# Codes read as they are loaded: the 4-bit levels of one core's second layer without a narrow copy

## What is computed

```python
x = x + _L0_ffn_ref(_L0_cond_ref(x, itok, L0_cond_weights), L0_ffn_w, L0_ffn_b)
x = x + _L1_ffn_ref(_L1_cond_ref(x, L1_cond_weights, itok), q_weight, q_scale, bias, lora_A, lora_B)
# in _L1_ffn_ref
w = NF4_LEVELS[q_weight].reshape(-1, GROUP_SIZE) * q_scale[:, None]
base = jnp.einsum('bsi,oi->bso', x, w) + bias
lora = jnp.einsum('bsr,or->bso', jnp.einsum('bsi,ri->bsr', x, lora_A), lora_B)
return base + SCALING * lora
```

## Time and profile before

| what | us |
|---|---|
| median of three executions | 372.79 |
| the three | 370.15, 373.74, 372.79 |
| the profiled execution, its own time | 371.03 |
| its span in the trace | 369.2 |
| busy in the span: PE, DVE, ACT, POOL | 354.6, 243.3, 169.6, 228.3 |

### The profile page before, as it was taken

One profiled execution on the slowest core, in us unless ns is written; L12 is line 12 of the kernel. 1 busy time (PEld: TensorE's weight loads), 2 busy tenths in 40 slices (PEclk: granted clock), 3 DMA queues, 4 the chain that ended last, 5 costly groups with the idle time before them and its releaser, 6 DMA issues.

```text
span 369.2 us, 5527 instructions
## 1 busy us (share of the span) xinstructions
PE 354.6 (96%) x1832; PEld 299.9 (81%) x1832; DVE 243.3 (66%) x361; ACT 169.6 (46%) x302; POOL 228.3 (62%) x147
## 2 busy tenths in 40 slices
PE   7999987999999999998989999999999999999996
PEld 6788875878888888887868888888888888888885
DVE  4996457587997887974699999846155362544522
ACT  4775647678888778882021323504013040231300
POOL 0769999956886878667443302386468464685642
PEclk9999999899999999999999999999999999999999
DMA  7994400554246146333331133021405014150202
GB/s 212 309 306 142 148 22 29 193 211 146 96 167 199 45 156 216 117 114 114 127 119 57 61 120 114 18 101 62 174 36 180 22 70 166 57 175 4 114 30 85
DMA packets 27838, 44.63 MB, mean 121 GB/s; under 512 B 8834, under 2 KB 17026, under 8 KB 27810
## 3 DMA queue, kind: packets, MB, share of 16 engines
q1 hardware_dynamic: 26466, 43.95, 34.9%
q10 hardware_dynamic: 1344, 0.33, 0.4%
HBM read 27.49 MB, written 16.78 MB: 120 GB/s over the span
## 4 chain that ended last, share of the span: by engine, by line
PE 73%; DVE 10%; ACT 6%; issue 4%; POOL 4%; DMA 1%; SPq 1%; DVEq 0%; POOLq 0%; ACTq 0%
PE acc L1177 31%; PE acc L1139 20%; PE xT L1103 9%; PE acc L1119 7%; PE spare L1103 3%; DVE plain_sums L927 3%; ACT spare L721 2%; POOL x_first L557 2%; DVE side_p L908 2%; DVE hl L865 2%; ACT hh L673 1%; PE acc L1204 1%; DMA mix<-in_L_cond_weights 1%; PE acc L1103 1%; POOL side_p L584 1%
## 5 line engine op out<-in xcount | busy, mean ns | idle before, releaser
L551 POOL TENSOR_TENSOR X<-X,bias 128x1024 f32<-128x1024 f32 x28 | 69.1, 2468 | 34.1 <-PE xT L1103 26.6
L1139 PE MATMUL acc<-T,hh 128*128 128x512 f32 x192 | 75.9, 396 | 0.0
L1139 PE MATMUL acc<-T,hl 128*128 128x512 f32 x192 | 75.0, 391 | 0.0
L721 ACT ACTIVATE spare<-q_mid 128x512 f32<-128x512 int8 x96 | 55.5, 596 | 13.6 <-DVE side_p L908 6.6
L1177 PE MATMUL acc<-W,hh 128*128 128x512 f32 x192 | 61.1, 389 | 0.0
L1103 PEld LDWEIGHTS xT<-mix,X 128*128 128x128 f32 x352 | 43.7, 197 | 7.4 <-issue 6.4
L1103 PE MATMUL xT<-mix,X 128*128 128x128 f32 x352 | 44.6, 282 | 4.2 <-DVE hl L865 4.1
L1010 DVE TENSOR_TENSOR X<-X,acc 128x512 f32<-128x512 f32 x36 | 24.7, 687 | 32.9 <-PE acc L1177 18.6
L1177 PEld LDWEIGHTS acc<-W,hh 128*128 128x128 f32 x192 | 36.0, 188 | 7.5
L1139 PEld LDWEIGHTS acc<-T,hl 128*128 128x128 f32 x192 | 36.1, 188 | 7.4
L1139 PEld LDWEIGHTS acc<-T,hh 128*128 128x128 f32 x192 | 36.1, 188 | 7.0
(11 more groups left out here) (97 smaller groups left out, 662.5 us busy)
## 6 DMA issues: line engine op xcount, KB each, us to landing
out<-X SPq DMA_DIRECT2D x26, 512.0 KB, 3.1
X<-out SPq DMA_DIRECT2D x16, 512.0 KB, 3.4
X<-in_x SPq DMA_DIRECT2D x12, 512.0 KB, 3.4
q_raw<-in_L_ffn_q_weight SPq DMA_DIRECT2D x16, 256.0 KB, 2.9
w_in<-in_L_ffn_w SPq DMA_DIRECT2D x15, 256.0 KB, 5.2
x_first<-in_x SPq DMA_DIRECT2D x4, 512.0 KB, 5.2
out<-x_first SPq DMA_DIRECT2D x4, 512.0 KB, 5.8
out<-X SPq DMA_DIRECT2D x4, 256.0 KB, 2.0
```

Of the source, the lines that this page charges most:

```text
L551: pool.tensor_tensor(x_of(g), x_of(g), bias[:, :], ALU.add).then_inc(s_xb, 1)
L721: act.activation(dst, q_mid[:, parity, :], ACT.Copy, scale=slope, bias=offset).then_inc(s_line, 1)
L1139: mm = pe.matmul(acc[:, bank_of(q), :], a[:, k, :], b, start=(k == 0 and j == 0), stop=(k == KB - 1 and j == len(terms) - 1))
```

## The change

ScalarE's lines read the 32-bit codes in `q_raw` instead of the one-byte copy; the copy, its two buffers and its semaphore `s_qmid` are gone. The lines are made for codes 0 to 15 instead of -7 to 8. For the first line of each side no slope and offset give both levels exactly at these codes, so that a small number is added to it on VectorE: the first maximum of a side becomes "add, then maximum with line 1", and the comparison with zero moves to the second maximum, which becomes the same kind of instruction as the first. The third maximum stays.

Two things follow in the order of the lists. ScalarE's whole becomes 8 instructions for each piece, and `share` cuts it at other places. And `q_raw` is now read by all eight lines, so `load_q(d)` waits until all lines of piece d - 2 are made (`s_line`) and no longer until its copy Q is made; and in SyncE's list it stands behind the spill and the load of X of its round, where it stood ahead of them.

```diff
             def load_q(d):
                 k, n = PIECES[d]
-                need(sp, s_qmid, d - 1)
+                need(sp, s_line, 2 * NL * (d - 1))
                 sp.dma_start(q_raw[:, d % 2, :, :], q_v[n, k]).then_inc(s_qin[d % 2], 16)
...
-            load_q(2)
+            for d in range(2, ND):
+                if ready_in(d - 2) < NH * F:
+                    load_q(d)
             for g in range(F, NT):
                 load_mix(g + 3)
-                for d in range(3, ND):
-                    if d > 3 and ready_in(d - 3) // NH == g or d == 3 and g == F:
-                        load_q(d)
                 if g == F:
                     for t in range(F):
                         spill(t)
                 else:
                     spill(g - 1)
                     load_x(g + 3)
+                for d in range(2, ND):
+                    if ready_in(d - 2) // NH == g:
+                        load_q(d)
...
-                    d, number = divmod(u, 2 * NL + 1)
+                    d, number = divmod(u, 2 * NL)
                     parity = d % 2
-                    number -= 1
-                    if number < 0:
+                    sign, j = divmod(number, NL)
+                    slope, offset = sides[sign][0][j]
+                    if number == 0:
                         act.wait_ge(s_qin[parity], 16 * (d // 2 + 1))
-                        need(act, s_line, 2 * NL * (d - 1))
-                        act.activation(q_mid[:, parity, :],
-                                       q_raw[:, parity, :, :].rearrange("p o i -> p (o i)"), ACT.Copy,
-                                       bias=-float(NF4_ZERO)).then_inc(s_qmid, 1)
-                        continue
...
-                    act.activation(dst, q_mid[:, parity, :], ACT.Copy, scale=slope, bias=offset
-                                   ).then_inc(s_line, 1)
+                    act.activation(dst, q_raw[:, parity, :, :].rearrange("p o i -> p (o i)"), ACT.Copy,
+                                   scale=slope, bias=offset).then_inc(s_line, 1)
...
-            per = (2 * NL + 1) * ND
+            per = 2 * NL * ND
...
+                    if j > 0:
+                        dve.wait_ge(s_max, v)
                     if j == 0:
+                        ins = dve.scalar_tensor_tensor(dst, dst, sides[sign][1], spare[:, c % LR, :],
+                                                       ALU.add, ALU.max)
+                    elif j == 1:
                         ins = dve.scalar_tensor_tensor(dst, dst, 0.0, spare[:, c % LR, :],
                                                        ALU.max, ALU.max)
                     else:
-                        dve.wait_ge(s_max, v)
                         ins = dve.tensor_tensor(dst, dst, spare[:, c % LR, :], ALU.max)
```

More of the change, by code:

```diff
@@ L66, in nf4_lines, with first_line @@
 def nf4_lines():
-    lv = [np.float32(x) for x in NF4_LEVELS]
+    f = np.float32
+    lv = [f(x) for x in NF4_LEVELS]
     z = NF4_ZERO
-    above = [line_through(k, lv[z + k], k + 1, lv[z + k + 1]) for k in (1, 3, 5, 7)]
-    below = [line_through(-k, -lv[z - k], -k - 1, -lv[z - k - 1]) for k in (1, 3, 5)]
-    below.append((-0.5, 1.0 - 0.5 * z))
-    for q in range(16):
[L78 to L82, removed]
+    def first_line(a, b):
+        want = abs(lv[a]), abs(lv[b])
+        middle = (float(want[1]) - float(want[0])) / (b - a)
+        for i in range(-8, 9):
+            slope = f(middle + i * float(np.spacing(f(abs(middle)))))
+            offset = f(-a * float(slope))
+            add = f(float(want[0]) - (a * float(slope) + float(offset)))
+            if all(f(f(q * float(slope) + float(offset)) + add) == w for q, w in zip((a, b), want)):
+                return (float(slope), float(offset)), float(add)
+        raise ValueError("no such line")
+    sides = []
+    for way in (1, -1):
+        line, add = first_line(z + way, z + 2 * way)
+        lines = [line]
+        for k in (3, 5, 7):
+            a, b = z + way * k, z + way * (k + 1)
+            lines.append(line_through(a, abs(lv[a]), b, abs(lv[b])) if b >= 0 else (-0.5, 1.0))
+        sides.append((lines, add))
+    for q in range(16):
+        value = []
+        for lines, add in sides:
+            first, *others = (f(q * float(f(s)) + float(f(o))) for s, o in lines)
+            value.append(max(f(first + f(add)), *others, f(0)))
+        assert value[0] - value[1] == lv[q], q
+    return sides
 def build(nc, x, itok, mix0, w0, b0, mix1, q_weight, q_scale, b1, lora_a, lora_b, out):
@@ L122, in build @@
     assert C * 2 == P and NH == 2 and ND == NT and G == 16 and R == 8
-    above, below = nf4_lines()
+    sides = nf4_lines()
     x_v = x.rearrange("(t s) c f -> t (s c) f", s=2)
@@ L216, in build @@
         q_raw = sb("q_raw", [P, 2, HB, P], I32)
-        q_mid = sb("q_mid", [P, 2, BANK], I8)
         side_p = sb("side_p", [P, SP, BANK], F32)
@@ L353, in build @@
         s_loraB = sem("s_loraB")
-        s_qmid = sem("s_qmid")
         s_line = sem("s_line")
```

## The result

| | before | after |
|---|---|---|
| median of 20 executions, us | 372.31 | 375.03 |
| lowest and highest, us | 369.63, 373.74 | 372.71, 377.68 |
| the profiled execution, its own time, us | 371.03 | 375.79 |
| its span, us | 369.2 | 374.0 |

The changed kernel takes 1.008 times as long as the kernel before (95% interval 1.0056 to 1.0103): 2.7 us more, where the sum said 1.9. The forecast was the right case and its size a little low. That the time lies in the stated range (370.0 to 377.5) says little by itself, as the range also holds the kernel before. That the steps of the forecast were not all right shows only in the trace.

The account below looks back on a forecast made before the run. TensorE was taken as the bound, busy 354.6 of 369.2 us, leaving 14.6 us idle to recover. Terms +2.4 and -0.5 gave +1.9 us, put on the 371.9 mean: 373.8 us, range 370.0 to 377.5.

Parts of the forecast that it names:

- the sum: Whole kernel: +2.4 us at piece 11 and -0.5 us at piece 15 make +1.9 us.
- The forecast: Main case: late codes at piece 11 make the kernel slower, 373.8 us likeliest; chance 0.5.
- Piece 11: Codes land at 130.2, wanted at 127.30; ScalarE stalls 2.9 us, TensorE waits 1.8 and 0.65: plus 2.4 us (1.4 to 3.4).
- the middle of two rows: Landing of codes behind one load of X: 3.7 us, between 2.7 alone and 4.7 behind two loads.
- Piece 7: Codes land at about 100.3, wanted at 98.9; the 0.9 us lag is used up ahead of `mixed(10)`: nothing.
- Piece 15: Codes land at 158.7, wanted at 157.50; TensorE's wait at 168.87 shrinks from 1.29 to 0.8 us: minus 0.5 us.
- The wait near 193 moves together: TensorE's last wait for a low part of x moves with all that is ahead; costed at nothing.
- the lines: ScalarE's lines on 32-bit codes: 2 ns more each, 0.3 us over 128; nothing on the path, at most 0.2 us.
- the maxima: One plain maximum per side becomes a three-operand instruction, 685 against 684 ns; 0.03 us over 32: nothing.
- the wait at 64: TensorE's 2.62 us wait at 63.94 for piece 1, behind GpSimd's first-layer sums, stays with its slow mixing instructions.
- The clock: Rival: granted clock falls after two new TensorE pauses near piece 11, 1.6 us more: +3.5 us, 375.4; chance 0.18.
- I had put it at 1.4: Rival, codes in time: no new stall, the 0.15 us sliver and 1.29 us wait go; -1.4 us, 370.5; chance 0.2.

Follow-up runs that it names:

- the kernel before with late loads: Kernel before with only SyncE's part of the change (code loads wait for all lines, stand behind spill and load of X): 379.18 us, ratio to before 1.0212.
- piece 11 ahead: Changed kernel with the load of codes of piece 11 alone moved ahead of its spill: 370.77 us, ratio to before 0.9979.
- piece 15 ahead: Changed kernel with the load of codes of piece 15 alone moved ahead of its spill: 371.74 us, ratio to before 0.9994.
- the first experiment: Changed kernel with seven loads of codes (pieces 3, 6, 7, 10, 11, 14, 15) ahead of spill and load of X: 367.98 us, ratio to before 0.9916.
- three buffers: Changed kernel with three buffers for the codes instead of two, loads still behind spill and load of X: 366.57 us, ratio to before 0.9863.
- all ahead: Changed kernel with all loads of codes ahead of the spill of their round: 367.38 us, ratio to before 0.9877.
- the last kernel: Kernel with three code buffers and GpSimd's piece 1 early, plus GpSimd's tile 16 addition waiting for VectorE's six block sums: 365.18 us, ratio to before 0.9797.

## Why the prediction was right, and where not

**Piece 11 was right in place, path and nearly in size.** ScalarE was to stand still for 2.9 us and stood 3.17; TensorE was to wait 1.8 and 0.65 us and waited 1.89 and 0.66. The codes took 3.93 us where the middle of two rows had said 3.7, and the spill's 2.62 was the 2.67 of the earlier trace rows. The times foretold (spill 123.4, codes 126.5) came 1.2 to 1.3 us late, at 124.7 and 127.7: that is the shift of piece 7.

By the prediction's estimate from the figures of the Trainium skill ("DMA: Bandwidth & Descriptors", Anatomy of one DMA), these codes would have landed in 3.4 us. The codes issued right behind one load of X took 3.7 to 3.9 us at six places of this trace and 5.3 at one, so the middle of the two rows was the nearer of the two.

**Piece 7 was wrong, and is the step that failed.** "Nothing" rested on codes that land at 100.3, a lag of 0.9 us and 1.5 us in hand. They landed at 101.85. The issue came when it should (96.55), but the tile ahead of the codes took 5.0 us and they themselves 5.30, as the issues of DMA in 96 to 97 us show, beside those in 127 to 129 us (KB each, median us to landing):

```profile
X<-in_x SPq DMA_DIRECT2D x1, 512.0 KB, 5.0
q_raw<-in_L_ffn_q_weight SPq DMA_DIRECT2D x1, 256.0 KB, 5.3
...
X<-in_x SPq DMA_DIRECT2D x1, 512.0 KB, 3.4
q_raw<-in_L_ffn_q_weight SPq DMA_DIRECT2D x2, 256.0 KB, 3.9
```

The range for a landing (2.7 to 4.7) was too narrow, and I had given it to piece 11 alone: already at 4.7 the codes of piece 7 come at 101.3, which is 2.4 us behind 98.9; less the 0.45 us for the copy that is gone, this is a lag of some 1.9 us, 0.4 more than the 1.5 in hand. ScalarE lost 2.93 us, TensorE 0.94 at 108.05, and starts behind it are 1.3 us later than before, where they were 0.1 us later near 77. Alone it measured 1.5 us.

It was not a chance event of one execution. With the same loads in the same place, the codes of piece 7 took 5.3, 5.3 and 5.5 us in the traces of the kernel before with late loads, of piece 11 ahead and of piece 15 ahead. The view of DMA packets in 96.5 to 98.5 us of the changed kernel shows one packet of another queue, which the profile names "instruction" (packets, MB, share of 16 engines):

```profile
q1 hardware_dynamic: 74, 0.30, 46.0%
q8 instruction: 1, 0.02, 3.9%
```

That is 1.25 us of one engine (3.9% of 16 engines in 2 us, an estimate), and the tile took 1.6 us longer than its 3.4 us elsewhere. Near 128, where the tile took 3.4 us, there is no such packet. Over all twelve traces (loads of X issued from 70 to 180 us), the loads of X with no such packet in flight took 3.0 to 3.8 us, all 117 of them; of the 14 with one in flight, 9 took 4.6 to 5.8. The codes that took 5.1 us or more, five in all, each had one in flight. So the packet goes with the long landings; that it causes them fits these numbers, but no run here moved it, and five of the 14 loads of X were not slowed.

**Piece 15 was right in its wait, and its "minus 0.5" partly by luck.** TensorE waited 0.98 us where 0.8 was foretold (1.29 before), so the wait shrank by 0.3. The starts moved forward by 0.55 in all (3.87 late at 141.00, 3.32 at 172.19), but 0.2 of that was won before this wait (3.70 late at 150.87), in a sliver that the prediction did not have. ScalarE stood still for 2.50 us ahead of P0, where 1.2 had been worked out (158.7 against 157.50); it came to P0 earlier than I had thought, and this cost nothing, since the landing of the codes set the time.

**"The wait near 193 moves together" was wrong as a rule.** In the changed kernel it does stay (1.96 against 1.78), in the first experiment and with piece 15 ahead it falls to 0.58 and 0.68. It hangs on how long GpSimd's addition has run when VectorE's first sum starts: 0.20 us in the kernel before, 0.03 in the changed one (184.30 and 184.33, and the sum took 2.92 us), 1.38 and 1.31 in the other two.

**What was counted at nothing and was nothing**: the lines (598 against 596 ns), the maxima (682 to 686 ns in all forms), the wait at 64 (2.65 against 2.62), no wait for codes at pieces 3, 6, 9, 10 and 14.

**The sum.** Worked out from starts of the same instruction in both traces, in the order of time:

| from | cause | us |
|---|---|---|
| piece 7 | idle 0.94 and what follows a pause | +1.2 |
| piece 11 | idle 1.89 and 0.66, and what follows | +2.6 |
| piece 15 | idle 0.98 in place of 1.29; a sliver near 147 gone | -0.5 |
| wait near 197 | 1.96 in place of 1.78 | +0.2 |
| to the end | the clock after 196, less small gains behind it | +1.3 |

That is 4.8, the difference of the spans. The first four make 3.5, where the prediction had 1.9: piece 7 is 1.2 of the difference.

**The clock** had a chance of 0.18 as a rival, as a fall behind the two new pauses. There the clock held: the mixing at 141.00 took 2.02 us. It fell after another one, at 196. And it is not a mark of the kernel but of an execution: over all executions, grouped by the mean granted clock of each (0.998 and more as 1.00, 0.994 with 0.995, 0.990 with 0.991), the times are

| mean granted clock | before | changed | first experiment |
|---|---|---|---|
| 1.00 | 369.7 (5) | 373.3 (4) | |
| 0.995 | 371.4 (26) | 374.5 (7) | 368.1 (6) |
| 0.991 | 372.7 (15) | 375.7 (7) | |
| 0.986 | 374.0 (5) | 376.7 (2) | |

(mean us, number of executions in brackets; those of before are from the runs beside the experiments, on three chips). Each step down costs 1.0 to 1.7 us. At the same clock the changed kernel is 2.7 to 3.6 us slower, near the 3.5 of the sum. Whether the clock falls after a given pause varies: in the profiles of the changed kernel and of "three buffers", the same pause of 2.65 and 2.66 us near 64 is followed by

```profile
62.00:72.00 10.00, 7.79 (x39) 6.99 (x40) 6.62 (x10) 6.12 (x11) 9.76 (x7) 0.83 0.42 137
```

in the one and by

```profile
62.00:72.00 10.00, 7.89 (x47) 6.92 (x48) 6.32 (x10) 6.86 (x13) 9.77 (x7) 1.00 0.41 133
```

in the other. With the pause cut to 0.2 and 0.9 us, 17 of 18 executions had a mean clock of 0.998 and more. What decides between a fall and none after the same pause stays open.

**What the change itself is worth** shows only with the codes in time: 3.4 to 5.1 us off (0.9916, 0.9877, 0.9863). Much of that spread is the clock: at the same mean clock the three kernels (seven loads ahead, all ahead, three buffers) are 2.9 to 3.5 us faster than the kernel before, and 6.4 to 6.6 us faster than the changed one. I had put it at 1.4, because I read the waits' idle times alone and left out what follows a pause, the collision near 180 and the clock.

## What to carry to other kernels

When a buffer is read by eight instructions where it was read by one, its next load moves later; follow every such load to its landing, through each transfer that stands ahead of it and with the longest landing in the trace, before the saved instructions are counted. If any lands later than its first reader wants it, put the load ahead of a spill that waits, or add a buffer, in the same change: here this turned 0.8% slower into 0.8 to 1.4% faster. And where the time of a kernel scatters with the granted clock, compare executions of the same mean clock, and count a pause that goes as more than its length.

## What the runs showed of the hardware

- A sum of two buffers of 128x512 on VectorE took 0.68 us alone. Where it began beside GpSimd's addition, it ended 0.5 us behind that one, so that it took 1.54 us behind a head start of 1.38 us and 2.73 to 2.92 behind one of 0.20 or less. GpSimd's addition took 2.4 us alone or when it began first, and 2.6 to 2.9 when a sum was under way. An addition of VectorE with one input in PSUM (`X<-X,acc`, 182.63 in the last kernel) took 0.69 us beside GpSimd. The Trainium skill ("SBUF — State Buffer", Who interferes with whom) says that a VectorE instruction with two inputs in SBUF contends with a GpSimd instruction that reads SBUF, and that the shared pair of ports is held as an exclusive lock; the trace agrees.
- A pause of TensorE costs a little more than its idle time: 0.94 us idle moved what follows by 1.2. In the same place the clock may or may not fall after it, and executions one step lower in mean clock were 1.0 to 1.7 us longer.
- 256 KB of codes right behind 512 KB of X took 3.7 to 3.9 us to land at six places of the changed kernel and 5.3 us at one, where a packet of the queue "instruction" was in flight; in all twelve traces no load of X issued from 70 to 180 us took over 3.8 us without such a packet, and 9 of 14 with one took 4.6 us or more. That the packet is the cause is not shown.
